# A graph network's first four passes: own rows scaled on ScalarE from fp32 rows kept in SBUF

## The reference, cut to what matters

```python
for _ in range(4):                                     # layer 0: passes 0 to 3
    transformed = einsum('nd,khd->knh', feat, W) + b   # 4 edge types
    a = segment_sum(transformed[etypes, src], dst)
    feat = gru_cell(a, feat, w_ih, w_hh, b_ih, b_hh)
x = layernorm(x + feat)
x = layernorm(x + gin(x, ...))                         # layer 1: passes 4 to 6
x = layernorm(x + batchnorm(relu(gcn(x, ...))))        # layer 2: pass 7
x = layernorm(x + sage(x, weight, ...))                # layer 3: pass 8
```

## Time and profile before

| | us |
|---|---|
| median of 3 runs | 9062.16 |
| lowest, highest | 9055.65, 9072.85 |
| the profiled execution | 9078.9 |
| its span, first to last instruction | 9076.7 |
| DVE busy | 7591.1 (84%) |
| PE busy | 6665.8 (73%) |
| POOL busy | 4813.9 (53%) |
| ACT busy | 2638.5 (29%) |

### The profile page before, as it was taken

The page is one execution under the profiler, slowest core; times in us unless marked ns, Lnnn a source line. Parts: engine busy times, 40 slices in busy tenths (PEclk is TensorE's granted clock), DMA queues, the critical chain, the costliest instruction groups (busy, mean ns, idle before and its releaser), DMA issues.

```text
span 9076.7 us, 299177 instructions
## 1 busy us (share of the span) xinstructions
PE 6665.8 (73%) x121341; PEld 5622.7 (62%) x121342; DVE 7591.1 (84%) x17381; ACT 2638.5 (29%) x6519; POOL 4813.9 (53%) x4224
## 2 busy tenths in 40 slices
PE   3666666658877888788777778876667777748888
PEld 1333333337777777777777767766666667737777
DVE  7988888868887998899788877867779978859998
ACT  0000000003333333333455543321123332234443
POOL 1333333335554564656444447868877767744443
PEclk8888888879999999999888889988889988969999
DMA  2211111136677777777655568988888888848887
GB/s 85 69 48 47 47 47 47 47 93 186 192 190 198 201 201 204 209 202 201 190 162 156 162 185 245 253 243 238 236 236 223 221 232 237 245 120 219 216 218 183
DMA packets 1157755, 1573.98 MB, mean 173 GB/s; under 512 B 407396, under 2 KB 850695, under 8 KB 1153466
## 3 DMA queue, kind: packets, MB, share of 16 engines
q1 hardware_dynamic: 916698, 898.54, 37.5%
q10 hardware_dynamic: 126656, 482.46, 15.2%
q0 software_dynamic: 113056, 174.29, 9.8%
HBM read 990.67 MB, written 564.09 MB: 171 GB/s over the span
## 4 chain that ended last, share of the span: by engine, by line
DVE 45%; PE 20%; DVEq 12%; DMA 9%; issue 9%; POOL 3%; ACT 2%; SPq 1%; ACTq 0%; POOLq 0%
DVE work L1983 7%; DMA work<-bounce_f 4%; DVE work L1958 3%; DMA bounce_f<-work 3%; DVE work L1939 3%; DVEq L1965 3%; POOL work L972 3%; DVE hs L1949 2%; DVE work L1745 2%; PE ps_gate L1244 2%; DVE work L1978 2%; PE ps_agg L1054 2%; DVE work L1866 2%; DVE hs L1737 2%; PE ps_agg L1183 2%
## 5 line engine op out<-in xcount | busy, mean ns | idle before, releaser
L972 POOL DMA_INDIRECT work<-node_rows,work x3528 | 4154.3, 1178 | 2753.9 <-issue 1254.4
L1183 PE MATMUL ps_agg<-work 120*128 120x64 bf16 (+1 forms) x12544 | 1394.9, 199 | 550.3 <-DVE work L1983 536.2
L1183 PEld LDWEIGHTS ps_agg<-work 120*128 120x128 bf16 x12544 | 1213.2, 102 | 599.8 <-issue 598.0
L1184 PE MATMUL ps_agg<-work 120*128 120x64 bf16 x12544 | 1392.6, 199 | 18.5 <-issue 18.0
L1185 PE MATMUL ps_agg<-work 120*128 120x64 bf16 x12544 | 1395.5, 199 | 11.5 <-issue 11.4
L1184 PEld LDWEIGHTS ps_agg<-work 120*128 120x128 bf16 x12544 | 1202.6, 102 | 35.6 <-issue 23.2
L1185 PEld LDWEIGHTS ps_agg<-work 120*128 120x128 bf16 x12544 | 1200.6, 101 | 18.2 <-issue 17.9
L1978 DVE TENSOR_TENSOR work<-work 120x1024 f32<-120x1024 f32 x784 | 956.3, 1220 | 305.1 <-DMA work<-bounce_f 301.6
L1152 PE MATMUL ps_pair<-rows_now,work 128*128 128x64 bf16 x26112 | 1008.6, 198 | 146.4 <-DMA work<-src_onehots 57.9
L1939 DVE TENSOR_TENSOR work<-iota_bf,dl_all 120x2048 bf16<-120x2048 bf16 x882 | 1075.0, 1219 | 15.3 <-POOL rows_now L998 7.3
L1205 PE MATMUL ps_agg<-work 128*128 128x64 bf16 (+1 forms) x23520 | 928.3, 195 | 178.1 <-DMA work<-node_rows,work 127.7
(11 more groups left out here) (345 smaller groups left out, 13037.5 us busy)
## 6 DMA issues: line engine op xcount, KB each, us to landing
bounce_f<-work ACTq DMA_DIRECT2D x816, 480.0 KB
work<-bounce_f SPq DMA_DIRECT2D x784, 480.0 KB
work<-src_onehots SPq DMA_DIRECT2D x918, 256.0 KB
bounce<-work ACTq DMA_DIRECT2D x102, 727.5 KB
work<-bounce SPq DMA_DIRECT2D x98, 727.5 KB
work<-node_rows,work POOLq DMA_INDIRECT x3528
work<-grid_vals SPq DMA_DIRECT2D x49, 960.0 KB, 5.0
node_rows<-stage SPq DMA_DIRECT2D x686, 48.0 KB
```

The source lines that it names most:

```text
L972: pool.indirect_dma_start(out=ring[:, at.slot6() * LB + b, 0:3 * H], out_offset=None, in_=table_of(at.p), in_offset=bass.IndirectOffsetOnA ...
L1183: mm(acc[:, to:to + n], hot, low[at.two()][0:ROWS, b, 0:n], start=b == 0, stop=False)
L1184: mm(acc[:, to:to + H], hot, tops(rest_f[at.two()])[0:ROWS, b, :], start=False, stop=False)
```

## The change

In passes 0 to 3 ACT makes the state and its scaled copies, in a new function `own_rows` that stands between `copy_turned` of t-1 and the tanh of the gates. It reads `xs` in pass 0 and `hs` in passes 1 to 3. So that `hs` holds the rows in fp32, `high` first copies the new row there in passes 0 to 2. DVE's `take_state` and the multiplication in `take_sums` go; a new semaphore, `own_scaled`, stands in front of the addition. The counts are copied by ACT in passes 1 to 3 and by DVE in pass 0. `normalize` of passes 3 and 6 writes its result straight into `xs`, in place of a buffer and a copy, and pass 3's parts are taken from `xs`.

```diff
+        def own_rows(at):
+            if at.p >= P_GIN1:
+                return
+            to, d = state[at.half()], at.d()
+            frm = xs if at.p == 0 else hs
+            a_(to[:, 0:H], frm[:, ds(d, 1), :].rearrange("p o f -> p (o f)"), ACT.Copy)
+            if at.p > 0:
+                a_(to[:, H:H + K + 1], counts[:, ds(d, 1), :].rearrange("p o k -> p (o k)"), ACT.Copy)
+            act.wait_ge(lrec_landed[at.slot6()], at.uses6(6) * 16)
+            act.sem_inc(act_ran, 1)
+            for k in range(K):
+                last = a_(agg_sb[:, k * H:(k + 1) * H], frm[:, ds(d, 1), :].rearrange("p o f -> p (o f)"), ACT.Copy,
+                          scale=lrec[at.slot6()][:, LB, k:k + 1])
+            last.then_inc(own_scaled, 1)
...
+            if p < 3:
+                a_(hs[:, ds(at.d(), 1), :], frm, ACT.Copy)
             a_(to[:, :, 0:H], frm, ACT.Copy).then_inc(hi_made, 1)
...
                 copy_turned(prev)
+            own_rows(at)
...
         def take_state(at):
-            if at.p < P_GIN1:
-                v.tensor_reduce(out=state[at.half()][:, 0:H],
-                                in_=tile(rows_now, at).rearrange("p (a f) -> p f a", a=3), axis=AX.X, op=ALU.add)
-            elif at.p < P_SAGE:
+            if P_GIN1 <= at.p < P_SAGE:
...
-                v.tensor_tensor(to, own_rec[:, 0:K].rearrange("p (k o) -> p k o", o=1).to_broadcast([P, K, H]),
-                                state[at.half()][:, 0:H].rearrange("p (o f) -> p o f", o=1).to_broadcast([P, K, H]),
-                                ALU.mult)
-                dve.drain()
-                v.tensor_tensor(to, to, typed[:, :, 0:H], ALU.add)
+                dve.wait_ge(own_scaled, at.tiles(1))
+                last = v.tensor_tensor(to, to, typed[:, :, 0:H], ALU.add)
...
-                last = v.tensor_copy(state[at.half()][:, H:H + K + 1], tile(counts, at))
+                if p == 0:
+                    last = v.tensor_copy(state[at.half()][:, H:H + K + 1], tile(counts, at))
...
-            to = {3: row[:, 0:H], P_GIN2B: o[:, :], P_SAGE: out_rows[:, at.kept(), :]}[p]
+            to = out_rows[:, at.kept(), :] if p == P_SAGE else tile(xs, at)
...
-            v.tensor_copy(tile(xs, at), to)
```

More of the change, by code:

```diff
@@ L402, in build @@
     sum_taken = sem("sum_taken")
+    own_scaled = sem("own_scaled")
     sum_turned = sem("sum_turned")
@@ L1485, in parts @@
             n = stores_of[at.p]
-            return stage[:, at.kept(), 0:n, :], row[:, 0:n * H].rearrange("p (n f) -> p n f", n=n), \
+            frm = row[:, 0:n * H].rearrange("p (n f) -> p n f", n=n)
+            return stage[:, at.kept(), 0:n, :], xs[:, ds(at.d(), 1), :] if at.p == 3 else frm, \
                 left_over[:, 0:n * H].rearrange("p (n f) -> p n f", n=n)
@@ L2016, in take_sums @@
                 if careful:
-                    v.tensor_tensor(agg_sb[:, :], agg_sb[:, :], more[:, 0:K * H], ALU.add)
+                    last = v.tensor_tensor(agg_sb[:, :], agg_sb[:, :], more[:, 0:K * H], ALU.add)
                     if p == 0:
@@ L2068, in parts @@
             n = stores_of[at.p]
-            return stage[:, at.kept(), 0:n, :], row[:, 0:n * H].rearrange("p (n f) -> p n f", n=n),                 left_over[:, 0:n * H].rearrange("p (n f) -> p n f", n=n), at.i * 6 + lo_before(at.p) + at.jj + 1
+            frm = row[:, 0:n * H].rearrange("p (n f) -> p n f", n=n)
+            return stage[:, at.kept(), 0:n, :], xs[:, ds(at.d(), 1), :] if at.p == 3 else frm, left_over[:, 0:n * H].rearrange("p (n f) -> p n f", n=n), at.i * 6 + lo_before(at.p) + at.jj + 1
         def rest_of(at):
```

## The result

| | us |
|---|---|
| before, median of 4 runs | 9060.19 |
| after, median of 4 runs | 8918.81 (8911.14 to 8922.1) |
| ratio after to before | 0.9841, 95% interval 0.9823 to 0.9858 |
| profiled execution after | 8918.49 (span 8916.3) |

The change takes 141 us off the median. It was forecast at 8867, 195 us less than the median of before, with a range of 8800 to 8975 that holds the measured time.

A forecast was written before the change was run, and what follows sets the result against it. Two side-by-side loops of nearly equal length, DVE's and one over PE and ACT, bound a step. 122 + 48 + 18 + 11 less 4 gives 195 us off the median 9062.16: 8867 us, 8-in-10 range 8800 to 8975.

The forecast's parts named there:

- The two loops: One tile step: DVE bounds the first half (0.58 us gained); PE and ACT bound the second (2.87 us), hiding the reduce.
- Own rows on ACT: Between L1451 and the gate's tanh: about 1.3 us of ACT copies per tile, hidden in passes 1 and 2.
- The cover: ACT's spare time between the end of own rows and PE being ready for the gate: 0.2 us.
- Rival B: Between L1451 and the gate ACT is late: no change (9062 us, chance 0.06) or slower (9156, chance 0.08).
- Rival C: Half the gain: N near 1.6, or the copy into hs holds back L2076 too long; 8960 us, chance 0.11.
- N: Time of own rows behind L1451's end on ACT: 1.2 us forecast; at 1.86 the 195 us are used up.
- gain 0.62: Passes 1 and 2, each step: 0.58 - 0.02 + 0.06 us, steps of 6.85 us, 122 us together.
- it keeps 0.1, so it doesn't become the bound: PE ahead of the transposes, passes 1 and 2: gives up 0.58 of its 0.69 us idle time.
- Pass 0: L2009 goes, the counts copy stays on DVE: 0.49 us a step, 48 us; bounds 0.1 to 0.8 a step.
- Pass 3: Own rows push ACT's table load, ACT becomes the bound; steps 9.2 to 9.5, taken 9.4 us: gain 18 us.
- Rival E: Pass 3: a drain ahead of the table load, 1.38 us longer each step, 135 us less gain; 9002, chance 0.03.
- Pass 6: DVE sets this pass; the copy into xs (L2063) goes, 0.11 us per tile, 11 us.

The follow-up runs named there:

- state-alone run: The kernel before, with ACT copying state and counts while the scaling by the own counts stays on DVE: 8992.76 us, ratio 0.9912.
- doubled run: The changed kernel with four more scaled copies per tile on ACT ahead of the four that count: 9079.12 us, ratio 1.0008 to the kernel before.
- short-stream runs: Source-row product as one matmul over 192 columns instead of three over 64, passes 0 to 7: kernel before 9050.42 us (0.9985), changed kernel 8794.19 us (0.9701).
- in-place edit: The kernel before, with only normalize writing straight into xs and the copy behind it gone, passes 3 and 6: 9052.03 us, ratio 0.9981.
- late run: The changed kernel with own rows moved behind the tanh of the gates: 8824.79 us, ratio 0.9733 to the kernel before.

## Why the prediction was right, and where its sizes were off

The two loops. Right: a typical step lost what lay in the first half and nothing of the reduce; the state-alone run shows it by itself (7.42 to 7.33, 0.34 us of DVE idle).

Own rows on ACT. The instruction durations and their overlap were right, 1.3 us in all, and they were hidden in passes 0 to 2. The cover was 0.35 instead of 0.2, shown by the doubled run. Rival B needed own rows to end 1.86 us behind the end of the copy ahead of them; 1.19 were measured (3139.32 to 3140.51). Rival C's wait of DVE for hi_made is there with its 0.2 us and costs nothing that can be told. (Its 8960 goes with N at 1.6; the sum written beside it, 44 and 20 to 40, gives 8931 to 8951.)

Passes 1 and 2, the term that was mis-sized: "gain 0.62" a step, 122 us. Measured 66. The step of "it keeps 0.1, so it doesn't become the bound" failed: I weighed PE's idle time against its work only in the step that I followed, and counted what is above the typical step (0.28 us of the mean) as lateness that stays. It was PE's stops for instructions, as far as the short-stream runs can tell them from stops for weight loads. They were 35 us in pass 2 before, mostly covered by waits of PE that the change removed, and 68 after, covered by less than half. With the short stream in both kernels this term is 130.

Pass 0: 58 instead of 48. Its mean step was 8.14 us in the kernel before and 8.08 with the in-place edit, which doesn't touch this pass; with the short stream 8.26; such scatter alone is worth 5 to 12 us.

Pass 3: 26 instead of 18. Right in kind: own rows push the table load and with it the gate, a full-clock step went from 8.82 to 9.02 (medians; forecast 9.22), and one in part at 1.2 GHz got shorter, from 9.97 to 9.57 (forecast 9.47). Their numbers moved too, which the forecast had not: 32 of the 97 steps were at full clock throughout before, 55 after; why is not shown. For a full-clock step the forecast is 0.2 us too long: I had left 0.14 us between the load and the gate, as in the earlier trace rows, but with the load as the last thing waited for it is 0.01 (4318.06, 4318.07). The 0.14 was still PE's: where PE ends the wait, the gate stands 1.91 to 1.93 us behind the start of the copy, in the late run's rows above as in the earlier trace rows. The rest is own rows, which started 0.37 us behind L1452 instead of 0.40 and were done 1.29 us later instead of 1.35. Rival E, a drain ahead of the load, is refuted: the load starts 0.02 us behind the last copy (4316.76, 4316.78). The Trainium skill, page "ScalarE: Activation LUTs", section "What ACT_TABLE_LOAD costs", counts a drain of about 1380 ns with each load. This trace contradicts that here: neither ahead of the load nor behind it is there room for one.

Pass 6: forecast 11 us. Its rows before and after (an addition once per tile, in turns on two buffers):

```profile
L2032 DVE SCALAR_TENSOR_TENSOR agg_sb<-delta,work,ps_agg x49: 279/280/282, 6698.2 to 7362.1; 128x64 f32<-128x64 f32 x49
L2032 DVE SCALAR_TENSOR_TENSOR agg_sb<-cand,work,ps_agg x49: 279/280/282, 6703.8 to 7369.1; 128x64 f32<-128x64 f32 x49
```

```profile
L2048 DVE SCALAR_TENSOR_TENSOR agg_sb<-delta,work,ps_agg x49: 279/281/282, 6553.6 to 7209.3; 128x64 f32<-128x64 f32 x49
L2048 DVE SCALAR_TENSOR_TENSOR agg_sb<-cand,work,ps_agg x49: 279/281/282, 6559.7 to 7214.5; 128x64 f32<-128x64 f32 x49
```

From the first start to the last it is 670.9 us before and 660.9 after, so 10 us. Passes 4 to 8 together gave 9.

The forecast of 8867 was 52 us too low. In the profiled executions passes 1 and 2 gave 56 us less than forecast and passes 0 and 3 gave 18 more, in part by scatter; that they made up for some of the miss is luck. The profiled execution of the kernel before also lay 19 us above its median, so the gain by medians is smaller than the 160 us of the rows.

## What to carry to other kernels

Work that is moved to a less busy engine costs by its place in that engine's queue: here 0.95 us per tile cost 150 us in total ahead of an instruction on the critical loop and 11 (at most some 40) behind it. Moving own rows one place down made the kernel faster than the change itself (0.9733 against 0.9841 of the time before), most of it in pass 3. And before a gain is multiplied by the number of steps, compare the mean step with the typical one: the difference is made of stops that may have been hidden by the very wait that the change removes.

## What the runs showed of the hardware

In a long written-out program TensorE stopped inside runs of equal matmuls, for up to 3.5 us, waiting for no semaphore, and went on 1.25 to 1.6 us behind the end of a 16384-byte packet of its instruction queue (more than 8 in 10 of the stops). The reading that it ran out of instructions rests on this and on the short-stream runs; what those leave open is said there. The stop at 3382 fell into a stretch (3382 to 3385) in which the DMA engines moved 43 GB/s on average, so load on them isn't needed for it. The Trainium skill, page "Runtime: NRT & Kernel Launch", section "Instruction fetch mechanics", says that instructions come in blocks of 16 KiB and that crossing a block is mostly hidden. The packet size agrees. Most crossings are hidden here too, but far from all: of some 119 packets in a pass, 26 and 31 came with a stop in passes 1 and 2 before, 40 and 49 after. After, that is 61 and 68 us in two passes of some 715 us, and at most some 8 us a pass once it has a fifth fewer packets. Why some packets are asked for so late stays open.
